# Narrow attention of a two-layer decoder: first scores ahead of the sums of the probabilities in three beats of four

## The chip, the core and the metric

One core of a Trainium2 chip (trn2) runs the whole decoder in one launch. The metric is the device time of that launch in microseconds, median of several runs. The core's engines have queues of their own, each in program order, and wait for each other through semaphores: TensorE (PE in the rows; PEld are its weight loads) multiplies, VectorE (DVE) and ScalarE (ACT) work on elements and may read the accumulators in PSUM, GpSimd (POOL) works on SBUF, SyncE (SP) issues DMAs.

## The reference, cut to what matters

A decoder of two layers on x of 64 batches x 128 tokens x 128 channels, with a context of 64 x 77 x 64. Its stages are a state-space scan, a self-attention with an MLP, a cross-attention with an MLP, a channel mix, a gated linear attention, the narrow cross-attention, and a layer of experts. The change lies in the narrow cross-attention: 16 heads of 8 channels, 77 context tokens:

```python
qh = (q @ Wq + bq).reshape(B, LQ, HEADS, D_K).transpose(0, 2, 1, 3)
kh = (k @ Wk + bk).reshape(B, LKV, HEADS, D_K).transpose(0, 2, 1, 3)
vh = (v @ Wv + bv).reshape(B, LKV, HEADS, D_K).transpose(0, 2, 1, 3)
scores = jnp.einsum('bhqd,bhkd->bhqk', qh, kh) * scale
attn = jax.nn.softmax(scores, axis=-1)
out = jnp.einsum('bhqk,bhkd->bhqd', attn, vh)
concat = out.transpose(0, 2, 1, 3).reshape(B, LQ, D_MODEL)
return concat @ Wo + bo
```

Its result is added to x and normalised, and the expert of each token is chosen in the same stage (argmax over 8 centroids).

## The kernel before, in words

Each stage is a phase with its own tiles and semaphores, and all engines meet at a barrier between phases. The narrow attention takes the 64 batches one by one, in a software pipeline of **beats**: `for t in BEATS` is unrolled in each engine's program, and in beat t each engine does a step of several batches. The order of the `if` lines in the loop is the order in that engine's queue; nothing reorders it. Batches come in groups of four (GROUP), so a beat's extra work follows from t modulo 4.

A batch n goes through these steps. TensorE makes its **first scores** (`first_scores`, L1399), queries by keys, 4 matmuls into four PSUM banks, two halves of two. VectorE takes the negative maxima of each bank (`maxima`, L1631), and splits them into two bf16 parts (`split`); TensorE turns them (`turn`, L1409), ScalarE copies that out (`turned`, L1560, tile nmT). Then TensorE makes the **second scores**, keys by queries with the maximum subtracted: 16 small matmuls add the maxima (L1421), 4 add the products (L1425), into the same four banks. ScalarE takes the exponential of two banks at a time (`probabilities`, L1546, tile pT). TensorE makes the **sums** of the probabilities (`sums`, L1436, 16 matmuls) and the **weighted** sums of the values (`weighted`, L1448, 16 matmuls). ScalarE inverts the sums (`inverse`: logarithm L1552, then exponential L1554, tile rinv), VectorE multiplies (`scaled`, L1639), TensorE projects (`project`, L1454), and VectorE adds the residual (`add`, L1648).

In beat t TensorE does second scores of batch t-2, project of t-4, the beat's extra work, sums of t-3, first scores of t+1, weighted of t-3 and turn of t. Since all batches share the four score banks, each step waits for the reader of the one before it. Second scores of t-2 wait, bank by bank, for the maxima of batch t (`max_ready`, L1417). First scores of t+1 wait, half by half, for the exponential of batch t-2, which is of the same beat (`exp_ready`, L1394). The extra work of TensorE is in beats with t % 4 = 0 `turn_x` (L1365) and `row_scores` (L1469), 1 `queries` (L1372) and `counts` (L1479 to L1482), 2 `context` (L1380, L1383), 3 `turn_row` (L1461), at the end of the beat. The steps that prepare a group run for t = 0 to 58, those of the experts (`row_scores`, `counts`, `turn_row`) from t = 11 on.

ScalarE does in beat t the exponential of t-2, the inverse of t-3, a beat's extra work, and the copy of turn's result: with t % 4 = 1 the extra work is the four masked queries (L1532, tile qm) and one more copy of them (L1534, tile qa), with 2 the keys (L1538), with 0 and 3 one copy each. `context` of TensorE waits for qa, since both use one bank.

Of the kernel before, what the change touches and what calls it, by code (L numbers as in the profile page):

```python
# [25 lines left out]
GROUP = 4  # L26
# [1190 lines left out]
def narrow_attention_phase(nc, env, name, wd, w):  # L1217
# [16 lines left out]
    with Phase(nc, name) as ph:  # L1234
# [87 lines left out]
        def there(n):  # L1322
            return 0 <= n < N

        def comes(t, p):

            g = t // GROUP + 1
            return g if t >= 0 and t % GROUP == p and g < NG else None
# [4 lines left out]
        def done(t, p, beats):  # L1333

            g = t // GROUP - beats
            return g if t % GROUP == p and 0 <= g < NG else None
# [17 lines left out]
        def _(pe):  # L1354
# [6 lines left out]
            def turn_x(g):  # L1361
                if g:
                    pe.wait_ge(v_ready, 2 * g)
                for b in range(GROUP):
                    mm = pe.transpose(pj[0][:, b * T:(b + 1) * T], X[:, g * GROUP + b, :], ident)  # L1365
                mm.then_inc(proj_mm, 1)

            def queries(g):
                pe.wait_ge(by_act, g * N_ACT + 1)
                if g >= 4:  # L1370
                    pe.wait_ge(pick_step, PICK * (g - 4) + 2)
                pe.matmul(pj[1][:, :], wq, xT[:, :]).then_inc(proj_mm, 1)  # L1372

            def context(g):
                pe.wait_ge(ctx_in[g % 2], 16 * (g // 2) + 16)
                pe.wait_ge(by_act, g * N_ACT + 6)
                if g >= 4:
                    pe.wait_ge(place, PLACE * (g - 4) + 1)
                for h in range(2):
                    mm = pe.matmul(pj[h][:, 0:VAL], wk[half(h), :], cT[half(h), g % 2, :])  # L1380
                for a in range(2):
                    for h in range(2):
                        mm = pe.matmul(pj[h][0:TK, VAL + a * P:VAL + (a + 1) * P], cT[half(h), g % 2, a * TK:(a + 1) * TK],  # L1383
                                       wv[half(h), :])
                mm.then_inc(proj_mm, 1)

            def first_scores(n):
                s, b = n // GROUP % 2, n % GROUP
                if b == 0:
                    pe.wait_ge(by_act, (n // GROUP + 1) * N_ACT)  # L1390
                pe.wait_ge(own_keys, n + 1)
                for two in range(2):
                    if n >= 3:
                        pe.wait_ge(exp_ready, 4 * (n - 3) + 2 * two + 2)  # L1394
                    elif n:
                        pe.wait_ge(max_ready, 4 * (n - 1) + 2 * two + 2)
                    for r in (2 * two, 2 * two + 1):
                        rows = slice(32 * r, 32 * r + 32)
                        mm = pe.matmul(sc[r][:, 0:4 * TK].rearrange("p (j t) -> p j t", j=4), qa[rows, s, b * T:(b + 1) * T],  # L1399
                                       km[rows, s, b])  # L1400
                    mm.then_inc(s1_mm, 1)

            def turn(n):
                pe.wait_ge(split_ready, 2 * (n + 1))
                if n:
                    pe.wait_ge(nmT_ready, n)
                if n >= 3:
                    pe.wait_ge(ln_ready, n - 2)
                pe.matmul(sb[:, 0:T], nsplit[:, :, :].rearrange("p r c -> p (r c)"), ident16[:, :]).then_inc(turn_mm, 1)  # L1409

            def second_scores(n):
                s, b = n // GROUP % 2, n % GROUP
                pe.wait_ge(nmT_ready, n + 1)
                for j in range(4):
                    for r in range(4):
                        if j == 0:
                            pe.wait_ge(max_ready, 4 * (min(n + 3, N) - 1) + r + 1)  # L1417
                            if n + 3 > N:
                                pe.wait_ge(exp_ready, 4 * (n - 1) + r + 1)
                        rows = slice(32 * r, 32 * r + 32)  # L1420
                        pe.matmul(sc[r][0:TK, j * T:(j + 1) * T], pick[rows, j, 0:TK], nmT[rows, b % 2, :],  # L1421
                                  start=(j == 0), stop=False)
                for r in range(4):
                    rows = slice(32 * r, 32 * r + 32)
                    mm = pe.matmul(sc[r][0:TK, :].rearrange("p (j t) -> p j t", j=4), kT[rows, s, b * TK:(b + 1) * TK],  # L1425
                                   qm[rows, s, :, b * T:(b + 1) * T], start=False, stop=True)
                mm.then_inc(s2_mm, 1)

            def sums(n):
                pe.wait_ge(exp_ready, 4 * n + 4)  # L1430
                pe.wait_ge(nmT_ready, min(n + 3, N))
                if n:
                    pe.wait_ge(ln_ready, n)
                for j in range(4):
                    for r in range(4):
                        mm = pe.matmul(sb[32 * r:32 * r + 32, T:2 * T], ones[0:TK, j, :], pT[0:TK, n % 2, r, j * T:(j + 1) * T],  # L1436
                                       start=(j == 0), stop=(j == 3))
                mm.then_inc(sum_mm, 1)

            def weighted(n):  # L1440
                s, b = n // GROUP % 2, n % GROUP
                if b == 0:
                    pe.wait_ge(v_ready, 2 * (n // GROUP) + 2)
                if n:
                    pe.wait_ge(out_read, n)
                for j in range(4):
                    for r in range(4):
                        mm = pe.matmul(ob[32 * r:32 * r + 32, 0:T], v[0:TK, s, b, r, 32 * j:32 * j + 32],  # L1448
                                       pT[0:TK, n % 2, r, j * T:(j + 1) * T], start=(j == 0), stop=(j == 3))
                mm.then_inc(pv_mm, 1)  # L1450

            def project(n):
                pe.wait_ge(oT_ready, n + 1)
                pe.matmul(ob[:, 0:C], oT[:, :], wo).then_inc(out_mm, 1)  # L1454
# [9 lines left out]
            def row_scores(g):  # L1464
                pe.wait_ge(xe_ready, g + 1)
                if g == 0:
                    pe.wait_ge(experts_loaded, 16)
                for b in range(GROUP):
                    mm = pe.matmul(pj[1][:, b * E:(b + 1) * E], xe[:, b * T:(b + 1) * T], cen)  # L1469
                mm.then_inc(score_mm, 1)  # L1470

            def counts(g):
                pe.wait_ge(pick_step, PICK * (g + 1))
                if g == 0:
                    pe.wait_ge(sorting, SORT)
                if g:
                    pe.wait_ge(place, PLACE * g)
                rows_of = lambda a, b: mine[:, g % 2, a:b, :].rearrange("p b e -> p (b e)")
                pe.matmul(pj[0][:, 0:GROUP * E], tri16[:, :], rows_of(0, GROUP), start=True, stop=False)  # L1479
                for d in range(1, GROUP):  # L1480
                    pe.matmul(pj[0][:, d * E:GROUP * E], ones16[:, :], rows_of(0, GROUP - d), start=False, stop=False)
                pe.matmul(pj[0][:, 0:GROUP * E].rearrange("p (b e) -> p b e", b=GROUP), ones16[:, :],  # L1482
                          bcast(so_far[:, g % 3, :], 1, GROUP), start=False, stop=True).then_inc(count_mm, 1)
# [6 lines left out]
            for t in BEATS:  # L1490
                if there(t - 2):
                    second_scores(t - 2)
                if there(t - 4):
                    project(t - 4)
                if g := comes(t, 0):
                    turn_x(g)
                if (g := done(t, 0, 3)) is not None:
                    row_scores(g)
                if g := comes(t, 1):
                    queries(g)  # L1500
                if (g := done(t, 1, 3)) is not None:
                    counts(g)
                if g := comes(t, 2):
                    context(g)
                if there(t - 3):
                    sums(t - 3)
                if there(t + 1):
                    first_scores(t + 1)
                if there(t - 3):
                    weighted(t - 3)  # L1510
                if there(t):
                    turn(t)
                if (g := done(t, 3, 2)) is not None:
                    turn_row(g)
# [1621 lines left out]
```

## Time and profile before

| | us |
|---|---|
| median of 3 runs | 3585.2 (3582.9 to 3586.72) |
| the profiled execution, its own time | 3584.1 |
| its span in the trace | 3582.3 |
| TensorE matmuls busy | 3274.7 (91%) |
| VectorE busy | 2394.3 (67%) |
| GpSimd busy | 2059.3 (57%) |
| ScalarE busy | 1978.5 (55%) |

The span is what the trace covers; the execution's own time is 1.8 us more. Busy shares are averages over nine phases; the narrow attention lies between 2941 and some 3345 us of the span. A row of a timeline gives the start, the time that the merged instructions cover, their number, and in brackets the idle time of their engine before them with what ended it. A float32 matmul of two passes can stand as two records, so that x8 is four matmuls.

### The profile page before, as it was taken

How to read it: one execution, taken by the hardware profiler on the slowest of the kernel's cores; microseconds unless marked ns; L12 is line 12 of the kernel's file. 1: busy time of each engine (PE TensorE's matmuls, PEld its weight loads, DVE VectorE, ACT ScalarE, POOL GpSimd, SP SyncE). 2: the span in 40 equal slices, each digit the busy share in tenths (PEclk: the TensorE clock that was granted, in tenths of full speed). 3: DMA queues.
4: the chain of work that ended last, by engine and by line, in shares of the span. 5: the costliest groups of instructions: out<-in, count | busy, mean ns of one | idle time of the engine just before them, and what ended most of it. 6: DMA issues, size and time to landing. Idle time of an engine off the chain costs nothing. (4 is left out here: it accounts for less than half of the span.)

```text
span 3582.3 us, 99654 instructions
## 1 busy us (share of the span) xinstructions
PE 3274.7 (91%) x39893; PEld 2049.4 (57%) x39893; DVE 2394.3 (67%) x5651; ACT 1978.5 (55%) x3574; POOL 2059.3 (57%) x1842
## 2 busy tenths in 40 slices
PE   6999999998899999898999999998999989999686
PEld 3554554454455555565666666775555545666575
DVE  5888888886455555476555555876777765666465
ACT  5666666663556666442566554435666646666354
POOL 4778877886577878664111112646777752433365
PEclk8999999999999999998999999999999999999798
DMA  4222222222900000000000000000000000000364
GB/s 140 87 88 89 89 86 88 81 84 99 316 23 2 2 2 2 16 1 12 4 5 5 5 4 6 1 8 8 2 2 2 2 16 18 26 17 15 90 175 118
DMA packets 50273, 164.52 MB, mean 46 GB/s; under 512 B 11823, under 2 KB 23218, under 8 KB 40785
## 3 DMA queue, kind: packets, MB, share of 16 engines
q1 hardware_dynamic: 45520, 150.43, 12.8%
q0 software_dynamic: 4352, 8.47, 0.7%
q8 instruction: 286, 4.69, 0.5%
q14 instruction: 115, 0.93, 0.1%
HBM read 149.89 MB, written 43.65 MB: 54 GB/s over the span
## 5 line engine op out<-in xcount | busy, mean ns | idle before, releaser
L504 DVE TENSOR_TENSOR_SCAN XC<-ssm_dA,ssm_db 128x2048 f32<-128x2048 f32 x128 | 565.4, 4418 | 110.0 <-PE ssm_db L359 97.4
L567 POOL TENSOR_TENSOR XC<-XC,XB 128x1536 f32<-128x1536 f32 x128 | 505.7, 3951 | 180.8 <-DVE XC L504 134.4
L373 PE MATMUL ssm_y<-XC,weights 128*128 128x512 f32 x1024 | 472.3, 604 | 2.5 <-POOL XC L567 2.3
L453 ACT ACTIVATE ssm_dA<-ssm_delta,ssm_nega 128x508 f32<-128x508 f32 x512 | 325.2, 707 | 84.1 <-DVE XC L504 83.6
L1193 POOL TENSOR_TENSOR self_pm<-self_pT,weights 128x512 f32<-128x512 f32 x256 | 322.9, 1298 | 63.1 <-ACT self_pT L922 61.6
L373 PEld LDWEIGHTS ssm_y<-XC,weights 128*128 128x128 f32 x1024 | 187.6, 191 | 215.6 <-issue 204.2
L1199 POOL TENSOR_TENSOR XC<-XC,XB 128x128 f32<-128x128 f32 x128 | 58.7, 459 | 400.1 <-DVE XB L1076 400.1
L2628 POOL TENSOR_TENSOR XC<-XC,weights 128x512 f32<-128x512 f32 x128 | 161.6, 1284 | 95.8 <-ACT XC L2462 95.8
L1062 DVE TENSOR_REDUCE self_nmax<-self_scores 128x4 f32<-128x512 f32 x256 | 158.4, 680 | 86.9 <-PE self_scores L802 86.9
L359 PEld LDWEIGHTS ssm_db<-XB,ssm_dxT 32*128 32x128 f32 x4096 | 135.9, 189 | 99.2 <-DVE XC L504 64.9
L359 PE MATMUL ssm_db<-XB,ssm_dxT 32*128 32x128 f32 x4096 | 161.7, 287 | 25.5 <-DVE XC L504 23.9
L2636 POOL TENSOR_TENSOR XC<-XC,weights 128x512 f32<-128x512 f32 x128 | 161.2, 1282 | 34.4 <-ACT XC L2471 34.2
L1631 DVE TENSOR_REDUCE narrow_nmax<-narrow_scores 128x4 f32<-128x308 f32 x256 | 104.5, 470 | 110.9 <-PE narrow_scores L1399 110.6
L922 ACT ACTIVATE self_pT<-self_scores 128x1024 f32<-128x1024 f32 x128 | 123.7, 1018 | 80.5 <-PE self_scores L828 54.7
L1884 PEld LDWEIGHTS mlp_yp<-weights,mlp_h 128*128 128x128 f32 x1024 | 133.2, 192 | 58.1 <-issue 56.4
L922 ACT ACTIVATE cross_pT<-cross_scores 77x1024 f32<-77x1024 f32 x128 | 123.6, 1015 | 72.2 <-PE cross_scores L828 58.9
L1546 ACT ACTIVATE narrow_pT<-narrow_scores 77x1024 f32<-77x1024 f32 x128 | 123.7, 1019 | 66.5 <-PE narrow_scores L1425 66.3
L1913 ACT ACTIVATE mlp_h<-mlp_hp,mlp_bias 128x512 f32<-128x512 f32 x128 | 88.0, 687 | 108.8 <-PE mlp_hp L1876 108.7
L1062 DVE TENSOR_REDUCE cross_nmax<-cross_scores 128x4 f32<-128x308 f32 x256 | 103.9, 466 | 57.5 <-PE cross_scores L802 57.5
L1876 PE MATMUL mlp_hp<-mlp_zT,weights 128*128 128x512 f32 x256 | 134.3, 611 | 1.5 <-ACT mlp_zT L1907 1.5
L1884 PE MATMUL mlp_yp<-weights,mlp_h 128*128 128x128 f32 x1024 | 134.2, 275 | 0.0
L2559 DVE TENSOR_TENSOR XC<-gla_scores,weights 128x512 f32<-128x512 f32 x128 | 82.1, 682 | 47.9 <-PE gla_scores L2334 47.7
(450 smaller groups left out, 8179.7 us busy)
## 6 DMA issues: line engine op xcount, KB each, us to landing
XB<-c_rows SPq DMA_DIRECT2D x64, 1024.0 KB
sorted<-in_padding SPq DMA_DIRECT2D x1, 33280.0 KB, 111.3
experts_we<-in_w_experts SPq DMA_DIRECT2D x72, 323.0 KB, 3.5
experts_rt<-sorted SPq DMA_DIRECT2D x72, 65.0 KB
ssm_xT<-in_xT SPq DMA_DIRECT2D x16, 256.0 KB
XC<-in_w_experts SPq DMA_DIRECT2D x9, 256.0 KB
weights<-in_w_self SPq DMA_DIRECT2D x1, 1412.0 KB, 7.2
cross_ctx_t<-in_ctx SPq DMA_DIRECT2D x16, 77.0 KB
```

Of the source, the lines that this page charges most:

```text
L359: mm = pe.matmul(of_batch(db, b)[:, :, 32 * c:32 * c + 32], dxT[rows, slot, half, c, :], diag(slot, c)[rows, nq, :].rearrange("p (k t) -> ...
L373: mm = pe.matmul(yp[half][:, :].rearrange("p (b t) -> p b t", b=GROUP), ident, of_state(states(32, at), k), start=(k == 0 and nq == 0 and ...
L453: o = act.activation(dA[:, p % 2, :].rearrange("p (b k t) -> p b k t", b=GROUP, k=4)[:, :, k, 1:T], by_batch(delta[:, slot, half, :])[:, : ...
L504: dve.tensor_tensor_scan(states(0, p).rearrange("p m t -> p (m t)"), dA[:, p % 2, :], db[:, :], 0.0, ALU.mult, ALU.add).then_inc(h_ready, 1)
L567: pool.tensor_tensor(states(32, p).rearrange("p (b k) t -> p b k t", k=4)[:, :, 0:3, :], states(0, p).rearrange("p (b k) t -> p b k t", k= ...
L922: act.activation(pT[0:TK, n % 2, 2 * i:2 * i + 2, :], scores[i][0:TK, :, :], ACT.Exp).then_inc(exp_ready, 2)
L1062: dve.tensor_reduce(nmax[:, r, :], sc[r][:, 0:4 * TK].rearrange("p (h t) -> p h t", h=4), AX.X, ALU.max, negate=True).then_inc(max_ready, 1)
L1193: pool.tensor_tensor(pm[:, n % 2, r, :].rearrange("p (h t) -> p h t", h=4), pT[:, n % 2, r, :].rearrange("p (h t) -> p h t", h=4), bcast(V ...
L1876: pe.matmul(hp[j][:, :], w2[:, j * P:(j + 1) * P], zT[:, g % 2, :]).then_inc(h_mm, 1)
L1884: mm = pe.matmul(yp[g % 2][:, b * C:(b + 1) * C], h[:, g % 2, j, b * T:(b + 1) * T], w3[:, j * C:(j + 1) * C], start=(j == 0), stop=(j == 3))
L2628: pool.tensor_tensor(a1(b, r), a1(b, r), bcast(tri, 1, 4), ALU.mult).then_inc(m1_pool, 1)
L2636: pool.tensor_tensor(a2(b, r), a2(b, r), bcast(tri0, 1, 4), ALU.mult).then_inc(m2_pool, 1)
```

## The change

In TensorE's loop the sums keep their place in front of the first scores in beats with t % 4 = 3. In the other beats they come behind the first scores. No other engine's program changes, no instruction is added or left out, and all waits stay with their steps.

```diff
@@ -1502,10 +1502,12 @@
                     counts(g)
                 if g := comes(t, 2):
                     context(g)
-                if there(t - 3):
+                if there(t - 3) and t % GROUP == 3:
                     sums(t - 3)
                 if there(t + 1):
                     first_scores(t + 1)
+                if there(t - 3) and t % GROUP != 3:
+                    sums(t - 3)
                 if there(t - 3):
                     weighted(t - 3)
                 if there(t):
```

TensorE's queue in one beat with t % 4 = 1, from the projection (L1454) behind the second scores to turn (L1409), before:

```order
L1454 MATMUL narrow_out<-weights,narrow_oT 128x128
L1372 MATMUL narrow_proj<-narrow_xT,weights 128x512
L1479 MATMUL narrow_proj<-narrow_mine,narrow_tri 128x32
L1481 MATMUL narrow_proj<-narrow_mine,narrow_ones 128x24
L1481 MATMUL narrow_proj<-narrow_mine,narrow_ones 128x16
L1481 MATMUL narrow_proj<-narrow_mine,narrow_ones 128x8
L1482 MATMUL narrow_proj<-narrow_so_far,narrow_ones 128x32
L1436 MATMUL narrow_sums<-narrow_pT,narrow_ones 32x128 x16
L1399 MATMUL narrow_scores<-XB,narrow_qa 128x308 x4
L1448 MATMUL narrow_out<-narrow_pT,narrow_v 32x128 x16
L1409 MATMUL narrow_sums<-narrow_ident,narrow_nsplit 128x128
```

and with the change:

```order
L1454 MATMUL narrow_out<-weights,narrow_oT 128x128
L1372 MATMUL narrow_proj<-narrow_xT,weights 128x512
L1479 MATMUL narrow_proj<-narrow_mine,narrow_tri 128x32
L1481 MATMUL narrow_proj<-narrow_mine,narrow_ones 128x24
L1481 MATMUL narrow_proj<-narrow_mine,narrow_ones 128x16
L1481 MATMUL narrow_proj<-narrow_mine,narrow_ones 128x8
L1482 MATMUL narrow_proj<-narrow_so_far,narrow_ones 128x32
L1399 MATMUL narrow_scores<-XB,narrow_qa 128x308 x4
L1436 MATMUL narrow_sums<-narrow_pT,narrow_ones 32x128 x16
L1448 MATMUL narrow_out<-narrow_pT,narrow_v 32x128 x16
L1409 MATMUL narrow_sums<-narrow_ident,narrow_nsplit 128x128
```

The sums (L1436) and the first scores (L1399) have changed places. What stands in front of both, projection, queries (L1372) and counts (L1479 to L1482), and behind both, the weighted sums (L1448) and turn, is as before.

The beat behind it (t % 4 = 2), from the projection on, before:

```order
L1454 MATMUL narrow_out<-weights,narrow_oT 128x128
L1380 MATMUL narrow_proj<-narrow_cT,weights 128x154 x2
L1383 MATMUL narrow_proj<-weights,narrow_cT 77x128 x4
L1436 MATMUL narrow_sums<-narrow_pT,narrow_ones 32x128 x16
L1399 MATMUL narrow_scores<-XB,narrow_qa 128x308 x4
L1448 MATMUL narrow_out<-narrow_pT,narrow_v 32x128 x16
L1409 MATMUL narrow_sums<-narrow_ident,narrow_nsplit 128x128
```

and with the change:

```order
L1454 MATMUL narrow_out<-weights,narrow_oT 128x128
L1380 MATMUL narrow_proj<-narrow_cT,weights 128x154 x2
L1383 MATMUL narrow_proj<-weights,narrow_cT 77x128 x4
L1399 MATMUL narrow_scores<-XB,narrow_qa 128x308 x4
L1436 MATMUL narrow_sums<-narrow_pT,narrow_ones 32x128 x16
L1448 MATMUL narrow_out<-narrow_pT,narrow_v 32x128 x16
L1409 MATMUL narrow_sums<-narrow_ident,narrow_nsplit 128x128
```

Here too the two have changed places, with context (L1380, L1383) in front of them. ScalarE's queue is the same in both programs; in the beats with t % 4 = 1 and 2 it is, from the exponential of the one to that of the next:

```order
L1546 ACTIVATE narrow_pT<-narrow_scores 77x1024 x2
L1552 ACTIVATE narrow_rinv<-narrow_sums 128x128
L1554 ACTIVATE narrow_rinv<-narrow_rinv 128x128
L1532 ACTIVATE narrow_qm<-narrow_proj,narrow_bias_q,narrow_scale_q 128x512 x4
L1534 ACTIVATE narrow_qa<-narrow_proj,narrow_bias_all 128x512
L1560 ACTIVATE narrow_nmT<-narrow_sums 128x128
L1546 ACTIVATE narrow_pT<-narrow_scores 77x1024 x2
```

The logarithm (L1552) waits for the sums, so everything below it in this queue is behind the step that moves on TensorE.

## Rows read from the trace of the kernel before

**Rows 1.** Busy us per engine (instructions), granted clock, DMA: ramp and steady narrow attention.

```profile
2941.00:2965.00 24.00, 20.41 (x256) 10.97 (x256) 12.62 (x36) 12.61 (x24) 7.85 (x10) 1.00 0.12 30
...
3100.00:3150.00 50.00, 48.64 (x882) 30.16 (x882) 31.37 (x120) 31.44 (x57) 19.54 (x25) 1.00 0.06 17
```

**Rows 2.** Waits of 2965 to 3320: us in total, times, longest us.

```profile
PEld narrow_scores L1421 <- DVE narrow_nmax L1631: 20.0, 85, 0.3
```

**Rows 3.** TensorE's timeline, a beat 1: start us, us, what, count.

```profile
3112.18 1.10 PE L1421 MATMUL narrow_scores<-narrow_nmT,narrow_pick 32*77 32x128 bf16 x16
...
3113.07 1.08 PE L1425 MATMUL narrow_scores<-narrow_qm,narrow_kT 32*77 32x512 f32 x8
...
3114.08 0.49 PE L1454 MATMUL narrow_out<-weights,narrow_oT 128*128 128x128 f32 x2
...
3115.48 1.08 PE L1436 MATMUL narrow_sums<-narrow_pT,narrow_ones 77*32 77x128 f32 x32
...
3116.49 0.80 PE L1399 MATMUL narrow_scores<-XB,narrow_qa 32*128 32x308 f32 x8
...
3117.22 1.08 PE L1448 MATMUL narrow_out<-narrow_pT,narrow_v 77*32 77x128 f32 x32
```

**Rows 4.** TensorE's timeline, heads of beat 2 and the next beat 3.

```profile
3118.39 1.10 PE L1421 MATMUL narrow_scores<-narrow_nmT,narrow_pick 32*77 32x128 bf16 x16
...
3124.56 0.55 PE L1421 MATMUL narrow_scores<-narrow_nmT,narrow_pick 32*77 32x128 bf16 x3
```

**Rows 5.** VectorE's timeline in that beat 1, with [idle before <- releaser].

```profile
3117.40 1.63 DVE L1631 TENSOR_REDUCE narrow_nmax<-narrow_scores 128x4 f32<-128x308 f32 x4 [2.46 <-PE narrow_scores L1399]
```

**Rows 6.** TensorE's timeline, a beat 3 and the beat 0 behind it.

```profile
3100.02 1.10 PE L1421 MATMUL narrow_scores<-narrow_nmT,narrow_pick 32*77 32x128 bf16 x16
...
3103.35 1.50 PE L1399 MATMUL narrow_scores<-XB,narrow_qa 32*128 32x308 f32 x8
...
3104.78 1.08 PE L1448 MATMUL narrow_out<-narrow_pT,narrow_v 77*32 77x128 f32 x32
...
3106.40 0.42 PE L1421 MATMUL narrow_scores<-narrow_nmT,narrow_pick 32*77 32x128 bf16 x16
...
3106.65 1.04 PE L1425 MATMUL narrow_scores<-narrow_qm,narrow_kT 32*77 32x512 f32 x8
...
3109.27 1.08 PE L1436 MATMUL narrow_sums<-narrow_pT,narrow_ones 77*32 77x128 f32 x32
```

**Rows 7.** ScalarE's timeline, beat 3, beat 1, the exponential of beat 2.

```profile
3102.08 1.93 ACT L1546 ACTIVATE narrow_pT<-narrow_scores 77x1024 f32<-77x1024 f32 x2 [1.67 <-PE narrow_scores L1425]
...
3114.24 1.93 ACT L1546 ACTIVATE narrow_pT<-narrow_scores 77x1024 f32<-77x1024 f32 x2 [1.67 <-PE narrow_scores L1425]
...
3116.63 0.28 ACT L1552 ACTIVATE narrow_rinv<-narrow_sums 128x128 f32<-128x128 f32 x1 [0.46 <-PE narrow_sums L1436]
...
3117.15 2.77 ACT L1532 ACTIVATE narrow_qm<-narrow_proj,narrow_bias_q,narrow_scale_q 128x512 f32<-128x512 f32 x4
...
3120.53 1.94 ACT L1546 ACTIVATE narrow_pT<-narrow_scores 77x1024 f32<-77x1024 f32 x2
```

**Rows 8.** Timeline in the ramp, first beat with sums.

```profile
2957.29 1.93 ACT L1546 ACTIVATE narrow_pT<-narrow_scores 77x1024 f32<-77x1024 f32 x2 [1.88 <-PE narrow_scores L1425]
...
2959.99 1.08 PE L1448 MATMUL narrow_out<-narrow_pT,narrow_v 77*32 77x128 f32 x32
```

**Rows 9.** TensorE's timeline, heads of t = 4, 8, 12, 60 and 63.

```profile
2961.16 0.42 PE L1421 MATMUL narrow_scores<-narrow_nmT,narrow_pick 32*77 32x128 bf16 x16
...
2984.32 0.42 PE L1421 MATMUL narrow_scores<-narrow_nmT,narrow_pick 32*77 32x128 bf16 x16
...
3007.91 0.42 PE L1421 MATMUL narrow_scores<-narrow_nmT,narrow_pick 32*77 32x128 bf16 x16
...
3303.07 0.42 PE L1421 MATMUL narrow_scores<-narrow_nmT,narrow_pick 32*77 32x128 bf16 x16
...
3319.81 0.42 PE L1421 MATMUL narrow_scores<-narrow_nmT,narrow_pick 32*77 32x128 bf16 x16
```

## Prediction

> **What bounds the kernel now.** I began with the table of busy time by stretches, to find the clock and the fullest engine of the narrow attention. In a steady 50 us TensorE is busy for 48.64 us at full clock, VectorE and ScalarE for about 31 each [rows 1]. So TensorE sets the pace, and the question is what its own instructions wait for. The table of waits answers it: 85 times the weight load in front of a second scores' matmul (L1421) waited for VectorE's maxima (L1631), 20.0 us in all [rows 2]. That is what this change aims at.
>
> Then the timeline, beat by beat. I name a beat by t modulo 4. Second scores open a beat, so beat lengths are differences between the first L1421 rows: beat 3 is 3100.02 to 3106.40 = 6.38, beat 0 to 3112.18 = 5.78, beat 1 to 3118.39 = 6.21, beat 2 to 3124.56 = 6.17; one group of four is 24.54 us [rows 3, 4, 6]. Unhindered, the 16 picks of L1421 take 3106.40 to 3106.65 = 0.25 us until L1425 starts [rows 6]. In beat 1 they take 3112.18 to 3113.07 = 0.89 us [rows 3]. The 0.64 us between is the wait for the maxima of first scores issued only a weighted sum earlier: VectorE starts them 0.18 us after that sum begins (3117.22, 3117.40) and needs 1.63 us, while the next second scores come 1.17 us after it (3118.39) [rows 3, 4, 5]. Beats 1, 2 and 3 open with this stall, since the beat before each has nothing else behind the weighted sum; beat 0 does not, since a group's last beat has turn_row there.
>
> **What the change removes.** In beats 0, 1 and 2 the first scores come ahead of the sums. The 16 matmuls of the sums (32 in the trace, 3115.48 to 3116.49 = 1.01 us, [rows 3]) then stand between the first scores and the next second scores, which are 2.18 us behind the sums' start (1.01 + 1.17). The maxima of the second half may start 0.18 us after the sums do and need half of 1.63, so they end near +1.0. The stall at the head of beats 1, 2 and 3 goes: 3 x 0.64 = 1.92 us a group. Nothing is added or removed on any engine, no DMA is issued by a moved step, and SP's and POOL's queues aren't passed.
>
> **What it costs: the exponential loses its cover.** First scores of batch t+1 write the banks that the exponential of batch t-2 reads: each half of them waits for one half of L1546. Second scores and exponential belong to the same beat. L1546 starts 1.17 us after L1425 (3113.07, 3114.24), so at 0.25 + 1.17 = 1.42 us into an unhindered beat [rows 3, 7]. What TensorE does when first scores wait for it, the trace shows in beat 3, where only project and the sums lie between: L1546 at 3102.08, the weighted sum at 3104.78, **2.70 us later** [rows 6, 7]. The first scores there stretch over 1.43 us in place of 0.73 (3116.49 to 3117.22), because the two halves no longer run side by side: the second can load only when both exponentials (1.93 us) are done, and then takes some 0.7 us by itself. In the ramp, in the first beat that has sums (no projection yet), the same distance is 2957.29 to 2959.99 = 2.70 [rows 7, 8]. Call it P. It holds wherever the next step would otherwise be ready before exponential + 2.70. After the change the natural start of the sums in beat 0 is 3109.27 - 3106.40 + 0.73 = 3.60, against 1.42 + 2.70 = 4.12 [rows 3, 6]; in beat 1 it is (3115.48 - 3112.18) - 0.64 + 0.73 = 3.39, against 4.12. So P decides in both, and each of these beats lasts 1.42 + 2.70 + 2.18 = **6.30 us**: beat 0 loses 0.52, beat 1 loses 0.09 in spite of its saved stall.
>
> **What is queued behind the later sums on ScalarE.** The logarithm L1552 waits for the sums, and ScalarE is in order. In beat 1 the four qm, qa and nmT stand behind it, and behind those the exponential of beat 2. Logarithm to that exponential is 3116.63 to 3120.53 = 3.90 us, with no idle time in it: ScalarE is already just in time here [rows 7]. The logarithm starts 1.15 us behind the sums' start (3115.48, 3116.63) [rows 3, 7]. Sums moved behind the first scores push this whole train. From beat 1's head: exponential 1.42, sums + 2.70, logarithm + 1.15, exponential of beat 2 + 3.90, its sums + 2.70, next beat's head + 2.18 = **14.05 us for beats 1 and 2**, against 12.38 before. Beat 2 alone becomes 7.75. Its context matmuls wait too, for qa to have read their bank, but that wait lies inside this chain. In other beats only short steps stand behind the logarithm. What waits for it elsewhere stays covered by the weighted sum: turn, which waits for it to have read the bank, comes 2.02 us behind the sums' start (1.01 twice), and the logarithm ends at 1.15 + 0.28; the reciprocal is through when qm starts, 0.52 after the logarithm, or 1.67, and VectorE's multiplication needs the weighted sum as well. Beat 3 keeps its order and only loses its stall: 6.38 - 0.64 = 5.74; its exponential + 2.70 is counted from its head, so it moves along.
>
> **The sum.** Group: 6.30 + 14.05 + 5.74 = 26.09, against 24.54: +1.55. Twelve groups (t = 12 to 59, 3007.91 to 3303.07, [rows 9]) are steady: +18.6. The two before have no row_scores in beat 0, so that beat loses more: t = 8 to 11 took 3007.91 - 2984.32 = 23.59 and will take 26.09, +2.50; the first took 2984.32 - 2961.16 = 23.16, and I take the same +2.5 (its beat 3 lacks turn_row both times): +5.0. The last three beats with first scores, without queries, took 3319.81 - 3303.07 = 16.74 [rows 9] and will take 3 x 6.30 = 18.90: +2.2. Together **+25.8 us**. TensorE is the pace of the phase, and phases are separated by barriers, so all of it shows. 3584.1 of the profiled execution + 25.8 = 3609.9. That execution is 1.1 us below the median of the runs, a difference that I leave aside: 3610.
>
> A different count comes from TensorE's idle share: 50 - 48.64 = 1.36 us in 50, or 0.67 a group [rows 1], as if only that could be won back, where I credit 1.92. By it the group would lose 1.55 + 1.25 = 2.80. But the 0.64 us sits inside a row that counts as busy [rows 3]. The Trainium skill, page Perfetto Trace Analysis, section Identifying the Most-Contended Engine, says just this: the matmul busy share is a poor measure of headroom. The trace agrees (0.89 us against 0.25 for the same 16 matmuls), and I credit 1.92.
>
> **Rivals.**
> *The second half is cheaper than P says (not slower).* If the sums could start as soon as both exponentials end, P would be 1.93 [rows 7], its lower bound: the second pair would stream beside them. Each group saves 3 x 0.77 = 2.31 of my cost: 1.55 - 2.31 = -0.76, by twelve -9.1; early groups 2 x 0.19 = +0.4, tail 2.2 - 2.3 = -0.1: -8.8, 3575. It turns to a gain below P = 2.70 - 1.55/3 = 2.18. Against it: both stalled places show 2.70, and weighted, the follower there, has the sums' shape. 4 in 100.
> *ScalarE's train is absorbed.* If beat 2's exponential kept 1.42, beats 1 and 2 would be 12.60, a group +0.10: 1.2 + 2 x 1.05 + 2.2 = +5.5, 3590, no change that can be told. Against it: no idle time in the train. 5 in 100. Something between this or the first and my sum (P a little shorter, part of the train absorbed): 3592 to 3602, 7 in 100.
> *Beat 3 keeps its stall*, because beat 2's maxima or VectorE's norm and values end late: 15 x 0.64 = +9.6 more, 3619.5. For it: VectorE has most to do there. Against it: 2.18 us from sums to second scores, where 1.0 is needed. 9 in 100.
> *The clock falls.* Beats now have waits of over 1 us. Were TensorE at half clock for one beat a group, some 5.5 us more each: 14 x 5.5 = 77, 3687. The rows speak against: 20.41 busy of 24 us at clock 1.00 in the ramp [rows 1], emptier than what I forecast ((24.54 x 0.97) / 26.09 = 0.91). The Trainium skill, page TensorE: Matmul & The Clock Gate, section A second HAM failure mode: psum-queue depth-cycling, tells of a clock that oscillates from short idles between groups; by that rule this rival would win. The ramp's row doesn't show it. 3 in 100.
>
> **Numbers.** My forecast has 72 in 100, with 3604 to 3616 as its own range. 3600 to 3620 takes in the stall that stays and the nearer part of the cases between, and leaves out under 2 in 10. A measurement tells about 0.2% (7 us) from nothing: faster 0.03 (the first rival), same 0.07 (part of it, and the second), slower 0.90.
>
> **What would show it.** A group of 26.1 us between L1532 starts; L1421 to L1425 0.25 in every beat; the wait of L1421 for L1631 gone from the table, and one of L1399 for L1546 in its place; in beat 2 L1546 starting 2.9 us after L1421 instead of 2.1, and context waiting for L1534. I am wrong if exponential to sums is well under 2.7, or if beat 2 is not the longest.

## The result: 63 us slower, and where they went

The changed kernel takes 3648.61 us (median; 3644.22 to 3658.96), the kernel before 3585.18; the ratio is 1.0177, 95% interval 1.016 to 1.0194. The forecast was 3610 with a range of 3600 to 3620: the sign is right, the size is not. The page of the changed kernel, span, first line of busy times, and the granted TensorE clock in 40 slices:

```profile
span 3642.3 us, 99654 instructions
...
PE 3321.9 (91%) x39893; PEld 2074.8 (57%) x39893; DVE 2402.2 (66%) x5651; ACT 1976.0 (54%) x3574; POOL 2058.3 (57%) x1842
...
PEclk9999999999999999998999999999999979889798
```

The phase lies in slices 33 to 38 (2941 to some 3400 us), and the clock there is not full throughout. The busy table has it by stretches, columns as in [rows 1]:

```profile
3000.00:3050.00 50.00, 46.35 (x760) 28.18 (x760) 26.79 (x96) 28.03 (x51) 11.19 (x15) 0.93 0.06 17
...
3100.00:3150.00 50.00, 48.37 (x767) 29.98 (x763) 27.21 (x96) 25.21 (x46) 16.18 (x19) 0.86 0.07 19
...
3200.00:3250.00 50.00, 46.86 (x743) 28.78 (x747) 28.71 (x108) 27.41 (x50) 16.34 (x20) 0.87 0.05 15
```

Clock 0.93, 0.86 and 0.87, where the kernel before had 1.00 [rows 1]. So two things are to be told apart: the order of the work at full clock, and the clock.

**The order, at full clock.** TensorE's timeline of a beat 1 and a beat 2 (the beat's head is L1421, as in [rows 3, 4]):

```profile
3119.05 0.42 PE L1421 MATMUL narrow_scores<-narrow_nmT,narrow_pick 32*77 32x128 bf16 x16
3119.31 1.04 PE L1425 MATMUL narrow_scores<-narrow_qm,narrow_kT 32*77 32x512 f32 x8
...
3121.67 1.57 PE L1399 MATMUL narrow_scores<-XB,narrow_qa 32*128 32x308 f32 x8
3123.17 1.08 PE L1436 MATMUL narrow_sums<-narrow_pT,narrow_ones 77*32 77x128 f32 x32
3124.07 1.06 PE L1448 MATMUL narrow_out<-narrow_pT,narrow_v 77*32 77x128 f32 x32
...
3125.22 0.42 PE L1421 MATMUL narrow_scores<-narrow_nmT,narrow_pick 32*77 32x128 bf16 x16
...
3128.29 0.53 PE L1380 MATMUL narrow_proj<-narrow_cT,weights 64*128 64x154 f32 x4 [1.36 <-ACT narrow_qa L1536]
...
3129.39 1.61 PE L1399 MATMUL narrow_scores<-XB,narrow_qa 32*128 32x308 f32 x8
3130.93 1.08 PE L1436 MATMUL narrow_sums<-narrow_pT,narrow_ones 77*32 77x128 f32 x32
...
3132.97 0.42 PE L1421 MATMUL narrow_scores<-narrow_nmT,narrow_pick 32*77 32x128 bf16 x16
```

and ScalarE's (two lines were put in, so that L1546 of before is L1548 here, L1552 is L1554, L1534 is L1536):

```profile
3120.47 1.93 ACT L1548 ACTIVATE narrow_pT<-narrow_scores 77x1024 f32<-77x1024 f32 x2 [1.04 <-PE narrow_scores L1425]
3124.32 0.28 ACT L1554 ACTIVATE narrow_rinv<-narrow_sums 128x128 f32<-128x128 f32 x1 [1.92 <-PE narrow_sums L1436]
...
3127.49 0.70 ACT L1536 ACTIVATE narrow_qa<-narrow_proj,narrow_bias_all 128x512 f32<-128x512 f32 x1
...
3128.22 1.93 ACT L1548 ACTIVATE narrow_pT<-narrow_scores 77x1024 f32<-77x1024 f32 x2
```

The picks take 0.26 us until L1425 (3119.05, 3119.31), not 0.89 as in [rows 3]: the wait for the maxima is gone. Exponential to sums is 3120.47 to 3123.17 = 2.70, and again 3128.22 to 3130.93 = 2.71. The logarithm now follows an idle of 1.92 us, the exponential of beat 2 comes 3.00 us behind the beat's head in place of 2.14 [rows 4, 7], and context (L1380) waits 1.36 us for qa. Beat 1 is 6.17 us, beat 2 7.75 us. The waits say the same for 2965 to 3380 us (total, times, longest):

```profile
PEld narrow_scores L1399 <- ACT narrow_pT L1548: 24.1, 55, 0.5
...
PE narrow_proj L1380 <- ACT narrow_qa L1536: 19.2, 14, 1.5
```

The row of L1421 for the maxima [rows 2] is no longer in that table.

**The clock.** Another beat 2 of the same trace and the head of its beat 3:

```profile
3177.22 0.42 PE L1421 MATMUL narrow_scores<-narrow_nmT,narrow_pick 32*77 32x128 bf16 x16
...
3180.29 0.53 PE L1380 MATMUL narrow_proj<-narrow_cT,weights 64*128 64x154 f32 x4 [1.36 <-ACT narrow_qa L1536]
...
3181.39 1.98 PE L1399 MATMUL narrow_scores<-XB,narrow_qa 32*128 32x308 f32 x8
3183.29 1.94 PE L1436 MATMUL narrow_sums<-narrow_pT,narrow_ones 77*32 77x128 f32 x32
3185.00 1.94 PE L1448 MATMUL narrow_out<-narrow_pT,narrow_v 77*32 77x128 f32 x32
...
3187.08 0.65 PE L1421 MATMUL narrow_scores<-narrow_nmT,narrow_pick 32*77 32x128 bf16 x16
```

Up to context it is the same beat. Then the first scores take longer, and the sums 1.94 us in place of 1.08. The busy table gives the granted clock from the head of the last beat 2 before this one to the end of the idle, and from the sums on:

```profile
3151.22:3180.29 29.07, 26.09 (x459) 16.09 (x458) 18.27 (x74) 18.51 (x35) 10.46 (x13) 1.00 0.05 14
3183.00:3188.60 5.60, 5.60 (x91) 3.79 (x89) 2.61 (x7) 1.27 (x4) 2.19 (x4) 0.50 0.01 3
```

The clock has gone from 1.00 to 0.50, that is from 2.4 to 1.2 GHz, behind an idle of 1.36 us and during the stretched L1399 (it falls some 2 us behind the end of the idle). The beat lasts 9.86 us. In this trace 6 of the 14 beats 2 (t = 6 to 58) are of this kind, in a second trace of the same kernel 8. After two of the six, the following beat 3 runs at half clock too and takes 9.18 us in place of 5.92.

From the head of t = 4 to the head of t = 63 the phase takes 3319.81 - 2961.16 = 358.65 us before [rows 9] and 3380.93 - 2965.80 = 415.13 us in the changed kernel (425.06 in its second trace). The experiment fill below has the same order of useful work at full clock and takes 382.59. So the order costs **+23.9 us** (my sum: 25.8), and the clock **+32.5** in one trace and +42.5 in the other. Beat by beat against fill, 25.6 of the 32.5 us lie in the six slow beats 2 and the beats right behind them, 2.7 in the last two beats, and 4.3 in t = 4 and 5, where the clock was still low from the entry (0.50 from 2945 to 2977 us, before any beat 2 had an idle for qa). In the second trace 35.9 lie in and behind the eight slow beats 2 and 6.9 in the last two beats. In the first trace the entry adds 4.6 us (head of t = 4 at 2965.80 for 2961.16), which isn't the change's: the program is the same up to there, and the second trace has that head at 2959.70. The 4.3 us behind it are of the same low stretch.

### The profile page after: what moved, and what is told of

Its sections match the earlier page's. It is cut to its first block and busy times, and to the rows that moved or that the text cites. A ratio compares the mean times of both kernels' runs of the same rounds, so it can differ in the third digit from the quotient of the medians.

```text
span 3642.3 us, 99654 instructions
## 1 busy us (share of the span) xinstructions
PE 3321.9 (91%) x39893; PEld 2074.8 (57%) x39893; DVE 2402.2 (66%) x5651; ACT 1976.0 (54%) x3574; POOL 2058.3 (57%) x1842
## 5 line engine op out<-in xcount | busy, mean ns | idle before, releaser
L1548 ACT ACTIVATE narrow_pT<-narrow_scores 77x1024 f32<-77x1024 f32 x128 | 123.5, 1017 | 63.3 <-PE narrow_scores L1425 63.3
```

## Experiments

Lengths of the four beats where the clock is full, read from the heads in each trace; "slow beats 2" are those of the 14 (t = 6 to 58) in which the clock was low in the trace; ratios are to the kernel before, beside which each ran, and can differ from the quotient of the medians by up to 0.0006:

| kernel | beat 0, 1, 2, 3 (us) | idle for qa in beat 2 | slow beats 2 | ratio, 95% interval |
|---|---|---|---|---|
| before | 5.79, 6.21, 6.17, 6.38 | none | 0, 0 | 1 |
| changed | 6.17, 6.17, 7.75, 5.92 | 1.36 | 6, 8 | 1.0177 (1.016 to 1.0194) |
| fill | 6.17, 6.17, 7.75, 5.92 | filled | 0 | 1.007 (1.0051 to 1.0089) |
| zero_two | 6.17, 5.53, 6.89, 5.92 | none | 0 | 1.0003 (0.9992 to 1.0013) |
| only_1 | 5.79, 6.80, 6.89, 6.37 | 1.36 | 1 | 1.0066 (1.0049 to 1.0082) |
| split_q | 6.17, 6.17, 6.43, 5.92 | none | 0 | 1.0017 (1.0008 to 1.0027) |
| one_two | 5.79, 6.81, 7.76, 5.91 | 1.36 | 6 | 1.0142 (1.0123 to 1.016) |
| zero_one | 6.17, 6.17, 6.89, 6.38 | 1.36 | 0 | 1.0049 (1.0031 to 1.0068) |
| fill_third | 6.17, 6.17, 7.76, 5.92 | about 0.9 | 3 | 1.0128 (1.0108 to 1.0148) |
| late_train | 5.79, 6.21, 7.34, 6.38 | 1.13 | 1 | 1.0053 (1.0033 to 1.0073) |
| half_only | 5.79, 5.93, 7.32, 5.92 | 1.27 | 5 | 1.0044 (1.0027 to 1.0062) |
| half_split | 5.79, 5.93, 5.98, 5.92 | none | 0 | 0.9964 (0.995 to 0.9978) |

**fill.** Is it the idle in beat 2 that brings the clock down?

```diff
             def project(n):
                 pe.wait_ge(oT_ready, n + 1)
+                if comes(n + 4, 2):
+                    for _ in range(3):
+                        pe.matmul(ob[:, 2 * T:4 * T].rearrange("p (a t) -> p a t", a=2), ident, bcast(ident, 1, 2))
                 pe.matmul(ob[:, 0:C], oT[:, :], wo).then_inc(out_mm, 1)
```

> The changed kernel with three extra 256-column float32 matmuls (about 1.3 us, into unused columns of the output bank, read by nobody) before the projection in each beat 2 of groups 1 to 15, where TensorE otherwise idles 1.36 us for qa. The order of all useful work is the changed one. Theory A (my schedule count of +25.8 us is right, and the rest of the loss is TensorE's clock, which falls because of that one long idle in beat 2): the clock stays at 1.00 between 3000 and 3300, a group takes 26.1 us, the time is 3605 to 3620. Rival B (the clock falls because of the many short waits of first scores for the exponential, in beats 0, 1 and 2 alike): the clock still falls to 0.9, 3635 to 3655. Rival C (the schedule costs more than I counted): 3640 to 3660 at full clock.

3613.41 us, ratio 1.007. Its TensorE rows in beat 2, from the head over the filler (L1456) to the sums, and a stretch of the busy table:

```profile
3184.37 0.42 PE L1421 MATMUL narrow_scores<-narrow_nmT,narrow_pick 32*77 32x128 bf16 x16
...
3185.59 1.56 PE L1456 MATMUL narrow_out<-weights 128*128 128x256 f32 x6
...
3187.44 0.53 PE L1380 MATMUL narrow_proj<-narrow_cT,weights 64*128 64x154 f32 x4
...
3188.54 1.61 PE L1399 MATMUL narrow_scores<-XB,narrow_qa 32*128 32x308 f32 x8
3190.07 1.08 PE L1436 MATMUL narrow_sums<-narrow_pT,narrow_ones 77*32 77x128 f32 x32
```

```profile
3150.00:3200.00 50.00, 49.33 (x860) 31.46 (x859) 31.55 (x116) 29.49 (x55) 16.88 (x21) 1.00 0.06 15
```

Context starts 3.07 us behind the head (3184.37, 3187.44), as without the filler (3125.22, 3128.29), the four beats are as long as in the changed kernel at full clock, and the clock is 1.00 in every stretch from 2965 to 3330. Work that nobody needs makes the kernel some 35 us faster (3648.61 to 3613.41). Theory A holds here: the order costs about what was counted, the rest is the clock, and with the gap of beat 2 filled it doesn't fall. The filler is matmul work as well as an absent idle; split_q below takes the idle away without it.

**zero_two, only_1, split_q.** The order's parts, one by one. In zero_two and only_1 the condition on t % GROUP picks the beats in which first scores go ahead; in the one, beats 0 and 2, in the other, beat 1:

```diff
-                if there(t - 3) and t % GROUP == 3:
+                if there(t - 3) and t % GROUP not in (0, 2):
                     sums(t - 3)
                 if there(t + 1):
                     first_scores(t + 1)
-                if there(t - 3) and t % GROUP != 3:
+                if there(t - 3) and t % GROUP in (0, 2):
                     sums(t - 3)
```

> First scores ahead of the sums in beats 0 and 2 only; beat 1 keeps sums first, so ScalarE's train (logarithm, queries, exponential of beat 2) isn't pushed and context doesn't wait. By my terms: beat 0 6.30, beat 1 6.21 - 0.64 = 5.57, beat 2 exponential at 2.14 + 2.70 + 2.18 = 7.02, beat 3 5.74: 24.63 a group against 24.54, about +4 us with early groups and tail: 3586 to 3593. Theory A: the clock stays at 1.00, so this is all. Rival B: short waits of L1399 for the exponential remain in two beats of four, and the clock falls in part: 3600 to 3625. A reader who holds each moved beat to cost the same would expect two thirds of the loss, +42: 3627.

3589.79 us beside 3589.13 of before: no difference, with the clock at 1.00 in every stretch from 3000 to 3300. Moving the step in two of the three beats costs nothing that can be measured, since the saved stall pays for the stretched first scores (a group takes 24.52 us beside 24.54). But this trace has one fall that doesn't fit theory A, in beat t = 60:

```profile
3294.92:3312.00 17.08, 16.63 (x263) 9.90 (x266) 11.90 (x44) 10.54 (x19) 8.96 (x11) 1.00 0.06 18
3313.00:3318.00 5.00, 5.00 (x72) 2.92 (x63) 1.78 (x10) 0.87 (x3) 0.00 (x0) 0.50 0.01 3
```

The beat takes 7.78 us for 6.17. From the head of t = 58 (3294.92) TensorE had no idle that its timeline shows, 0.45 us in 17.08 in all, and three stretched first scores in a row (beats 2, 3 and 0). The same three were stretched in every group before (beat 0's by less, 1.32 us for 1.61, but in t = 8 1.61 too) without a fall.

> First scores ahead of the sums in beat 1 only. By my terms: its own beat 2.06 + 2.70 + 2.18 = 6.94 (+0.73), ScalarE's train pushed to 2.87 us into beat 2, whose context waits about 1 us for qa and which lasts 2.87 + 2.70 + 1.17 = 6.74 (+0.57); group 25.84, +1.30, +19 us in all. Theory A: TensorE's idle of 1 us in beat 2 is there, so the clock falls too, and the time is 3625 to 3645. Rival B: few short waits, the clock stays: 3600 to 3610.

3612.06 us, ratio 1.0066. The order's count is right (25.85 us a group, 25.84 expected), and theory A fails: the idle is there and the clock holds in all but one beat 2.

```profile
3182.52 0.53 PE L1380 MATMUL narrow_proj<-narrow_cT,weights 64*128 64x154 f32 x4 [1.36 <-ACT narrow_qa L1536]
3182.86 0.63 PE L1383 MATMUL narrow_proj<-weights,narrow_cT 64*77 64x128 f32 x8
3183.42 1.08 PE L1436 MATMUL narrow_sums<-narrow_pT,narrow_ones 77*32 77x128 f32 x32
3184.43 0.80 PE L1399 MATMUL narrow_scores<-XB,narrow_qa 32*128 32x308 f32 x8
```

Here dense sums follow context, and the first scores behind them aren't stretched (0.80 us). The idle alone isn't enough.

The edit of split_q is on ScalarE: `queries` is cut in two, and its first two copies are issued in front of `inverse`:

```diff
+                if g := comes(t, 1):
+                    first_queries(g)
                 if there(t - 3):
                     inverse(t - 3)
...
                 if g := comes(t, 1):
                     queries(g)
```

> The changed kernel, with ScalarE's queries of beat 1 split: two of the four qm copies run before the logarithm, where ScalarE is idle for 1.92 us waiting for the sums, and two and qa behind it. Nothing else moves. By my terms the train shortens by 2 x 0.69 = 1.38: the exponential of beat 2 starts at about 1.5 us instead of 2.9, context no longer waits, beat 2 takes 6.37 instead of 7.75, a group 24.71, +6 us in all: 3588 to 3596 if theory A holds and the clock stays at 1.00. Rival B: the short waits of L1399 are all still there, so the clock falls as before: 3610 to 3635.

3594.06 us, ratio 1.0017. Beat 2 takes 6.43 us for 7.75, the idle is gone, and no beat 2 is slow, although first scores still wait for the exponential as in the changed kernel (57 times, 24.6 us, between 2965 and 3320). This one edit on another engine gives back all but 0.2% of the 1.8%: most of the loss came by ScalarE's queue, and rival B (the short waits alone) doesn't explain the falls in beat 2. That short waits never bring the clock down isn't shown: see t = 60 in zero_two.

**one_two, zero_one, fill_third, late_train.** What must stand beside the idle? The first two change the beats in the same two conditions, to (1, 2) and (0, 1). fill_third is fill with `range(1)`. late_train has the order of before, and in front of the queries on ScalarE:

```diff
                 act.wait_ge(proj_mm, g * NJ + 2)
+                for i in range(2 if g >= 2 else 0):
+                    act.activation(idle_out[:, :], xT[:, :], ACT.Identity).then_inc(idled, 1)
+                    act.wait_ge(idled, 2 * (g - 2) + i + 1)
```

> First scores ahead of the sums in beats 1 and 2, beat 0 as before. In beat 2 the 1.36 us idle for qa is followed at once by first scores that wait for the exponential, as in the changed kernel. By the beats measured so far at full clock: 5.79 + 6.80 + 7.75 + 5.92 = 26.26 a group against 24.54, about +25 us. Theory D (the clock falls where the long idle and the stretched first scores stand back to back in beat 2): falls occur behind beats 2 as in the changed kernel, 3630 to 3650. Rival E (it takes the waits of all three beats together): the clock holds, 3605 to 3615.

3640.9 us, ratio 1.0142, six slow beats 2.

> First scores ahead of the sums in beats 0 and 1, beat 2 as before: the idle of 1.36 us for qa is there, but dense sums follow context before the first scores. Full-clock beats: 6.17 + 6.17 + 6.89 + 6.38 = 25.61, +1.07 a group, about +18 us. Theory D: the clock holds, 3600 to 3612. Rival E: two beats of waits and the long idle, the clock falls in part: 3615 to 3640.

3607.35 us, ratio 1.0049, no slow beat 2, though the same idle stands in each. The pair differs most in beat 2: with the idle and then stretched first scores the clock falls, with the idle and then the sums it holds.

> The changed kernel with one extra 256-column float32 matmul (about 0.43 us) instead of three before the projection of each beat 2; the idle for qa shrinks from 1.36 to about 0.9 us. The schedule is the same, 26.0 us a group at full clock. Theory D with the length of the idle mattering: fewer falls or none, 3608 to 3625. If 0.9 us followed by stretched first scores is as bad as 1.36: 3640 to 3655.

3634.02 us, ratio 1.0128, three slow beats 2: a shorter idle, fewer falls, and still some. A third of the filler isn't enough; how much would be wasn't tried between one and three matmuls.

> The kernel before with its order, and two extra ScalarE copies of 512 columns (about 1.3 us with their waits, result read by nobody) in front of the queries of beat 1, so that ScalarE's train is as late as in the changed kernel while the sums stand in front of the first scores in all beats. If the pushed train is what costs: context waits about 1 us for qa in beat 2, the exponential of beat 2 starts at about 3.4 us, the beat takes 7.3 instead of 6.17, about +16 us: 3597 to 3606, clock at 1.00 by theory D (dense sums follow the idle). Rival: the train has slack that I don't see, and nothing changes, 3583 to 3590.

3609.96 us, ratio 1.0053. With the sums in front everywhere, a ScalarE train that is late brings the same wait:

```profile
3192.70 0.53 PE L1382 MATMUL narrow_proj<-narrow_cT,weights 64*128 64x154 f32 x4 [1.13 <-ACT narrow_qa L1539]
3193.04 0.63 PE L1385 MATMUL narrow_proj<-weights,narrow_cT 64*77 64x128 f32 x8
3193.60 1.08 PE L1438 MATMUL narrow_sums<-narrow_pT,narrow_ones 77*32 77x128 f32 x32
```

Beat 2 takes 7.34 us (7.3 expected). So the late train brings the idle and the longer beat by itself, whatever the order on TensorE. One beat 2 of 14 was slow here, which the theory of the pair doesn't exclude and doesn't foresee.

**half_split and half_only.** If the sums are both the cover of the exponential and, behind the first scores, that of the maxima, they can be halved. half_only:

```diff
-                if there(t - 3) and t % GROUP == 3:
-                    sums(t - 3)
+                if there(t - 3):
+                    sums(t - 3, range(4) if t % GROUP == 3 else range(2))
                 if there(t + 1):
                     first_scores(t + 1)
                 if there(t - 3) and t % GROUP != 3:
-                    sums(t - 3)
+                    sums(t - 3, range(2, 4))
```

with `for j in part` in `sums`, and the increment of sum_mm in the second half only. half_split has ScalarE's split queries of split_q besides.

> Made from what was measured: in beats 0, 1 and 2 the first 8 of the 16 sums' matmuls stand in front of the first scores and the other 8 behind them, and ScalarE's four qm copies are split around the logarithm as before in this study. The first half covers the exponential, the second half covers the maxima. By my terms: beats 0 and 1 last 1.42 + 2.70 + 0.50 + 1.17 = 5.79 (before 5.78 and 6.21), beat 2 with its exponential at 1.49 lasts 5.86 (before 6.17), beat 3 5.92 (before 6.38): 23.36 a group, -1.18, or -15 us in all, at clock 1.00: ratio 0.995 to 0.997. If halving the sums costs a break in TensorE's flow, or a stall for the maxima stays, the ratio is 0.998 to 1.001.

3574.83 us, ratio 0.9964 (0.995 to 0.9978): faster than both kernels. Its beats 0 and 1 on TensorE:

```profile
3171.49 0.42 PE L1421 MATMUL narrow_scores<-narrow_nmT,narrow_pick 32*77 32x128 bf16 x16
...
3174.36 0.65 PE L1436 MATMUL narrow_sums<-narrow_pT,narrow_ones 77*32 77x128 f32 x16
3174.94 0.80 PE L1399 MATMUL narrow_scores<-XB,narrow_qa 32*128 32x308 f32 x8
3175.67 0.65 PE L1436 MATMUL narrow_sums<-narrow_pT,narrow_ones 77*32 77x128 f32 x16
3176.13 1.06 PE L1449 MATMUL narrow_out<-narrow_pT,narrow_v 77*32 77x128 f32 x32
...
3177.28 0.67 PE L1421 MATMUL narrow_scores<-narrow_nmT,narrow_pick 32*77 32x128 bf16 x16
...
3180.14 0.65 PE L1436 MATMUL narrow_sums<-narrow_pT,narrow_ones 77*32 77x128 f32 x16
3180.71 0.96 PE L1399 MATMUL narrow_scores<-XB,narrow_qa 32*128 32x308 f32 x8
3181.60 0.65 PE L1436 MATMUL narrow_sums<-narrow_pT,narrow_ones 77*32 77x128 f32 x16
3182.06 1.06 PE L1449 MATMUL narrow_out<-narrow_pT,narrow_v 77*32 77x128 f32 x32
...
3183.21 0.51 PE L1421 MATMUL narrow_scores<-narrow_nmT,narrow_pick 32*77 32x128 bf16 x16
```

First scores take 0.80 and 0.96 us, hardly stretched, and the picks behind them 0.67 and 0.51 for 1.10. A group takes 23.62 us, 0.92 less than before (1.18 expected): a small stall for the maxima is left at beat 1's head (0.45 us until L1425, for 0.25) and the exponential of beat 2 starts 1.67 us behind its head, for 1.49 counted.

> The sums in two halves around the first scores in beats 0, 1 and 2, ScalarE's queue as before. The train from the logarithm to the exponential of beat 2 is then still pushed, by about 0.7 us against beat 2's head, and context waits for qa: 5.79 + 5.79 + 7.24 + 5.92 = 24.74 a group, +0.2, or +4 us at full clock: 3588 to 3594 beside 3585 of before. The long idle in beat 2 is followed by half the sums and then by stretched first scores; if the clock falls there as it does in the changed kernel, some 3600 to 3615.

3606.27 us, ratio 1.0044: 31 us more than half_split for want of the split queries. The order's part is 24.96 us a group for 24.54; the rest is the clock, low in 5 of 14 beats 2. Half the sums stand between the idle and the stretched first scores there, and the clock still falls.

**after_again and before_again**, a second trace of either kernel.

> The changed kernel unchanged, for a second trace. If the falls of the clock come from beat 2's idle, this trace has some 5 to 8 beats 2 of over 9 us out of 15, at other places than the first; every beat at full clock repeats within 0.1 us (6.17, 6.17, 7.75, 5.92).

3649.95 us. 8 slow beats 2 of 14, five of them at places where the first trace has none; the beats at full clock are those of the first trace.

> The kernel before unchanged, for a second trace. If the low clock between 2941 and 2965 us in the changed kernel's trace belongs to the change, this trace has 1.00 there as the first had; if the entry into the phase varies by itself, it can have 0.6 to 0.9 with the head of t = 4 up to 4 us later.

3582.52 us, clock 1.00 from 2941 to 3330, head of t = 4 at 2959.14. Its beats repeat those of the first trace within 0.02 us. The entry varies by itself in the other kernels (heads of t = 4 from 2959.70 to 2969.20), all of which have the same program up to there. The granted clock of 2941 to 2965 us was 1.00 in four of the fourteen traces (before twice, the second of the changed kernel, half_split) and 0.55 to 0.86 in the other ten. Why it differs isn't shown.

## Why the prediction was wrong

**What held.** The stall at the heads of beats 1, 2 and 3 went (0.26 us for 0.89). P, exponential to sums, was 2.70 and 2.71 for 2.70. ScalarE's train behind the logarithm was pushed as counted: beats 1 and 2 take 13.92 us for 14.05 forecast. A group takes 26.01 us for 26.09, and the whole order +23.9 us for +25.8. Two errors of size in it nearly cancel: the sums are 0.90 us from the weighted sum where they were taken at 1.01 (3123.17, 3124.07), so beats 0 and 1 are 6.17 for 6.30; and beat 3 is 5.92 for 5.74, since the weighted sum waits for VectorE there (8 waits of 4.6 us in all before L1448, put down to the copy of the values L1616, with the addition L1650 queued behind it). The first rival (P down to 1.93) and the second (train absorbed) are refuted by these rows; the third, the whole stall staying in beat 3, too.

**What failed** is the step on the rival "The clock falls": the sum held TensorE at full clock for the whole phase, a term of 0 us, and gave the fall 3 in 100. The clock cost 32.5 and 42.5 us, more than the whole forecast loss. I argued from a busy share: the ramp was at full clock with 20.41 of 24 us busy, emptier than my forecast of 0.91. That row doesn't carry the argument, for two reasons. First, it doesn't hold for its own program. This is the same stretch, of programs that are the same up to t = 4, first in the trace of fill, then in the second one of the changed kernel, columns as in [rows 1]:

```profile
2941.00:2965.00 24.00, 20.99 (x197) 10.11 (x198) 12.88 (x35) 10.21 (x18) 7.82 (x10) 0.72 0.12 30
...
2941.00:2965.00 24.00, 20.43 (x256) 10.60 (x260) 14.91 (x40) 11.88 (x21) 7.83 (x10) 1.00 0.12 30
```

The granted clock of it was 0.55 to 0.86 in ten traces of fourteen. That both traces of the kernel before had 1.00 there was luck for the argument. Second, a busy share doesn't tell a fall from none: in the 52.18 us before one of its falls (3125.22 to 3177.40) the changed kernel was busy for 48.93, or 0.94, while only_1 was at 0.93 (46.51 of 50) and its clock held. A stretched L1399 counts as busy while it waits, which I had said of L1421 in the same prediction and didn't apply here. What the runs show in place of the share is a sequence: idle of 1.36 us, short work, and then first scores that wait twice.

The rival's price of one fall was near; its chance and the number of falls weren't. By the traces a fall costs 1.8 to 2.4 us in beat 2, 0.8 to 3.3 in the beat 3 behind it, and 1.0 to 2.2 in the next beat 0 where it lasts that long: 4.3 us a fall in the first trace (25.6 for six) and 4.5 in the second (35.9 for eight), for my 5.5. I had priced every group and got 77; six and eight of fourteen fell. With the clock of the two traces my sum would have been 3642 or 3652.

**How far the cause is settled.** Shown: without the idle no beat 2 is slow (fill, zero_two, split_q, half_split, 0 of 56 beats, and 0 of 28 in the two traces of before); with the idle and stretched first scores right behind context 20 of 42 are (changed twice, one_two); with the idle and all the sums in between 2 of 42 (only_1, zero_one, late_train). half_only lies between (5 of 14). The Trainium skill, page TensorE: Matmul & The Clock Gate, section A second HAM failure mode: psum-queue depth-cycling, tells of short idles between groups of matmuls that make the clock oscillate; the traces agree with it, in that no wait of TensorE in the changed kernel is longer than 1.5 us between 2965 and 3380 us. The idle isn't the only way down: zero_two fell in t = 60 without one, and in the changed kernel, one_two, only_1 and fill_third the clock also fell in t = 61, behind the last beat 2. Open: why one such beat falls and the next doesn't, what exactly the chip counts, why the entry is at low clock in most traces, and why half_only's half of the sums doesn't help.

## What to carry to other kernels

A step on the bound engine often covers two waits at once, one before it and one behind it; moving it trades one for the other, and halving it can keep both. Before moving it, follow who waits for it on an in-order engine, to the last instruction behind: here four copies for another purpose carried the delay into the next beat, and splitting them took away most of the loss. And where a change leaves a repeated idle on TensorE followed by work that waits (0.9 to 1.36 us was enough here), forecast the half clock too, and don't rule it out by one row of one trace; cheap filler in the gap tells whether it is the clock.

## What wasn't expected of the hardware

TensorE's granted clock went from 1.00 to 0.50 behind single idles of 1.36 us, in a phase that is over 90% busy by its records. Two traces of one program had 6 and 8 such beats, mostly at different places, and in zero_two the clock fell once with no idle before it. Stretches of the same program in the entry were at 1.00 in four traces and at 0.55 to 0.86 in ten. The four runs of the changed kernel spread over 14.7 us (3644.22 to 3658.96) and the four of the kernel before beside them over 3.8, but later sets of the kernel before (7 to 19 runs) spread over 10.4 to 11.6, so this spread says little.
